# Windowed attention on pairs of tiles in four row groups, keys spread by DMA, and an expert pipeline with one more stage

## The reference

```
x = x + attention(layernorm(x))     # 16 heads of 8, token i sees tokens i-31 .. i
x = x + ffn(layernorm(x))
attention: qkv = h @ W_qkv + b_qkv; softmax(q k^T / sqrt(8), window 32) v; @ W_out + b_out
ffn:       shared expert: (h @ ws_up * silu(h @ ws_gate)) @ ws_down, for every token
           router: softmax(h @ w_router) over 8; only the first choice counts;
           choices 0 to 6: + 2 * p * ((h @ w_up[e] * silu(h @ w_gate[e])) @ w_down[e])
           choice 7: nothing is added
```

## Time and profile before

| | us |
|---|---|
| median of 3 runs | 367.87 (359.6 to 368.02) |
| the profiled execution | 365.89, its span 364.2, mean granted clock 0.986 |
| first find_max to the end of the last weigh_values | 21.6 to 151.2 |
| scatter on POOL begins | 176.9 |
| experts' first full step to the last | 247.9 to 349.2 |

### The profile page before, as it was taken

How to read it: one execution, slowest core, us unless ns; L and a number is a source line. 1 busy time by engine, 2 the same in 40 slices (tenths; PEclk the granted TensorE clock), 3 DMA queues, 4 the chain that set the end, 5 groups by cost and what they waited for, 6 DMA issues and landing times. The chain is left out here.

```text
span 364.2 us, 12603 instructions
## 1 busy us (share of the span) xinstructions
PE 323.2 (89%) x4976; PEld 251.8 (69%) x4976; DVE 226.5 (62%) x539; ACT 173.5 (48%) x313; POOL 175.6 (48%) x256
## 2 busy tenths in 40 slices
PE   8878999989889888997794799998899999999980
PEld 8645665655646555796682688876788888888870
DVE  4975888888788978779552133344555555555540
ACT  1646657557556755854231122233455445445530
POOL 6652456464446646785477244463333334333331
PEclk9999999999999999999999899999999999999996
DMA  8964433333443321000013111132343443433200
GB/s 205 354 226 126 123 104 99 100 98 97 133 119 103 99 50 38 4 2 0 22 54 114 50 61 60 63 65 67 60 77 74 79 75 66 80 74 69 62 17 0
DMA packets 56844, 30.68 MB, mean 84 GB/s; under 512 B 27073, under 2 KB 53189, under 8 KB 56787
## 3 DMA queue, kind: packets, MB, share of 16 engines
q1 hardware_dynamic: 53216, 23.18, 25.7%
q0 software_dynamic: 2880, 6.43, 5.1%
q10 hardware_dynamic: 690, 0.26, 0.4%
HBM read 13.72 MB, written 11.95 MB: 70 GB/s over the span
## 5 line engine op out<-in xcount | busy, mean ns | idle before, releaser
L608 POOL DMA_INDIRECT out<-y,xn_base x38 | 37.5, 986 | 69.9 <-DVE y L1220 69.9
L1233 DVE TENSOR_TENSOR Pr<-psS,PT 128x256 f32<-128x256 f32 x76 | 28.7, 420 | 41.4 <-issue 29.5
L892 DVE TENSOR_REDUCE row_max<-psS 128x16 fp32r<-128x1024 f32 x32 | 39.1, 1224 | 17.7 <-PE psS L1294 17.7
L1036 DVE TENSOR_TENSOR hT<-psS,PT 128x512 f32<-128x512 f32 x32 | 22.1, 690 | 40.7 <-PE psO L1456 20.5
L777 ACT ACTIVATE PT<-psS 128x512 f32<-128x512 f32 x32 | 19.1, 597 | 57.3 <-PE psS L1444 24.9
L1580 PEld LDWEIGHTS psB<-down_sb,Pr 128*128 128x128 f32 x304 | 39.6, 191 | 5.5 <-issue 2.4
L437 POOL TENSOR_TENSOR rows<-rows,proj 128x128 f32<-128x128 f32 x31 | 14.1, 456 | 57.3 <-ACT proj L686 54.8
L1580 PE MATMUL psB<-down_sb,Pr 128*128 x304 | 40.2, 275 | 1.8 <-DVE y L1220 1.0
L928 DVE STREAM_TRANSPOSE PT<-Pr 128x1024 f32<-128x1024 f32 x32 | 39.6, 1236 | 2.6 <-ACT Pr L680 2.4
L1323 PEld LDWEIGHTS psO<-VD,PT 128*32 128x32 f32 x2048 | 22.4, 109 | 25.0 <-issue 24.5
L1323 PE MATMUL psO<-VD,PT 128*32 128x36 f32 x2048 | 26.6, 200 | 10.8 <-DMA VD<-V 7.0
(11 more groups left out here) (200 smaller groups left out, 724.2 us busy)
## 6 DMA issues: line engine op xcount, KB each, us to landing
sorted_rows<-pad_row SPq DMA_DIRECT2D x19, 264.0 KB
VD<-V SPq DMA_DIRECT2D x120, 36.0 KB, 2.4
xn_base<-sorted_rows SPq DMA_DIRECT2D x38, 66.0 KB
xs<-sorted_rows SPq DMA_DIRECT2D x152, 16.0 KB
rows<-in_L_attn_x SPq DMA_DIRECT2D x8, 256.0 KB, 5.7
gate_sb<-in_L_ffn_w_gate SPq DMA_DIRECT2D x1, 1792.0 KB, 10.3
up_sb<-in_L_ffn_w_up SPq DMA_DIRECT2D x1, 1792.0 KB, 14.9
down_sb<-in_L_ffn_w_down SPq DMA_DIRECT2D x7, 256.0 KB
```

Source lines behind the costliest of these rows:

```text
L608: pool.indirect_dma_start(out=out_list, out_offset=bass.IndirectOffsetOnAxis(tok_u[:, r, :], 0), in_=y[:, r, :], in_offset=None, bounds_ch ...
L892: nc.vector.tensor_reduce(row_max[:, k % 2, :], s, AX.X, ALU.max).then_inc(max_done, 1)
L1233: nc.vector.tensor_tensor(hs[:, r % 2, h], psS[:, r % 2, h], sg[:, r % 2, h], ALU.mult).then_inc(done, 1)
```

## The change

**Pairs and row groups.** Attention goes by pairs of tiles. The queries are evicted once. Head h of each group of 4 now lies on partitions h, h+4, ... of the group's 32 (a permuted copy of the weights, `wqk_sb`), and each score matmul uses 32 rows and 32 columns of the array, so that 16 tiles of the array are named in turn. A pair has 16 mask matmuls and 32 score matmuls, over all four banks of `psS`. The next pair's scores wait for both exponentials of this one.

**Keys.** From the second batch on ACT evicts the keys once into `K`, and four DMAs on SP copy each head's rows into `Kx`, whose other rows stay zero. A batch's first scores wait for them (`k_in`).

**SP's order.** Downs and padding leave the places between the spreads and stand behind the last one: 10 padding DMAs (the last is shorter), then the 7 downs. The padding's source is made by POOL in the memory of V, once all spreads have landed.

**PE's order** in a pair, and the experts': a whole gate and up of tile s, then the transposes of s-1, then down of s-2.

```diff
-                for v in range(2):
-                    last = nc.scalar.activation(
-                        Qx[:, odd, v, :], psA[:, :], ACT.Identity, bias=bq_of[:, v : v + 1], scale=pair_of[:, v : v + 1]
-                    )
+                nc.scalar.activation(
+                    Qx[:, odd, :], psA[:, :], ACT.Identity, bias=bqk_sb[:, 0:1], scale=1.0
+                ).then_inc(q_ready, 1)
...
+            def evict_k(n, odd):
+                act.wait_ge(k_done, n + 1)
+                if n > 0:
+                    if n > 1:
+                        act.wait_ge(k_in, 16 * HPG * (n - 1))
+                    nc.scalar.activation(
+                        K[:, :], psB[:, :], ACT.Identity, bias=bqk_sb[:, 1:2], scale=1.0
+                    ).then_inc(k_ready, 1)
+                    return
...
+            def spread_keys(n):
+                sp.wait_ge(k_ready, n + 1)
...
+                for h in range(HPG):
+                    sp.dma_start(Kx[h::HPG, n % 2, h, BLK:], K[h::HPG, :]).then_inc(k_in, 16)
...
-            for n in range(B):
-                for half in range(2):
-                    spread_values(n, half)
-                    load_or_pad()
-                    load_or_pad()
+            spread_values(0, 0)
+            spread_values(0, 1)
+            for n in range(1, B):
+                spread_keys(n)
+                if n > 1:
+                    spread_values(n - 1, 1)
+                spread_values(n, 0)
+            spread_values(B - 1, 1)
+            sp.wait_ge(pad_ready, 2)
+            for lo in range(0, MT, PADS):
+                write_pads(lo, min(lo + PADS, MT))
+            for e in range(NE):
+                load_down(e)
...
+            mm(psB[:, 0:2], by_dim[:, :], bqkv_sb[:, 0:2], start=True, stop=True).then_inc(bqk_mm, 1)
...
+            act.wait_ge(bqk_mm, 1)
+            nc.scalar.copy(bqk_sb[:, :], psB[:, 0:2]).then_inc(bqk_ready, 1)
+            act.wait_ge(bqk_ready, 1)
             normalise_first()
...
+                for t in range(TPP):
                     for j in range(NJ):
-                        at = k * P + j * BLK
-                        for t in range(2):
-                            r = slice(2 * t * BLK, 2 * (t + 1) * BLK)
...
+                        at = (h * TPP + t) * P + j * BLK
+                        for g in range(NG):
+                            r = slice(g * BLK, (g + 1) * BLK)
                             last = mm(
...
+                                psG[j * BLK : (j + 1) * BLK, g, t * HPG * KEYS : (t + 1) * HPG * KEYS],
+                                Qx[r, b % 2, at : at + BLK], Kx[r, b % 2, :, at : at + KEYS],
+                                start=False, stop=True, skip_group_check=True,
                             )
...
+            for p in range(NP):
+                find_max(p, 0)
+                find_max(p, 1)
+                if p > 0:
+                    output(p - 1)
+                turn_probs(p, 0)
+                turn_probs(p, 1)
...
+            for s in range(1, MT):
+                expert_gate(s, s, at[s])
+                expert_up(s, s, at[s])
+                if s + 1 < MT:
+                    [at[s + 1]] = weights_of(s + 1)
+                expert_turn(s - 1, s - 1)
+                if s >= 2:
+                    expert_down(s - 2, s - 2, at.pop(s - 2))
```

More of the change, by code:

```diff
@@ L756, in batch @@
[L756 to L768 removed]
+                if p > 0:
+                    evict_proj(p - 1)
@@ new lines, in pair @@
+                if n < B and h == 0:
+                    evict_q(n, odd, first=n < 2)
+                if n + 1 < B and h == 1:
+                    evict_xnT(n + 1)
+            for p in range(NP - 3):
+                pair(p)
+            normalise_rows(3, 1)
+            pair(NP - 3)
+            normalise_rows(4, 1)
+            turned_batch(0)
+            turned_batch(1)
+            pair(NP - 2)
+            turned_batch(2)
+            turned_batch(3)
+            pair(NP - 1)
+            turned_batch(4)
@@ L982, in batch, with turn_probs @@
-            def batch(b, first=False, last=False):
-                for k in range(TPB):
-                    tile(b, k, first=first, last=last)
-            find_max(0, 1, first=True)
-            batch(0, first=True)
-            for b in range(1, B - 1, 2):
-                batch(b)
-                batch(b + 1)
-            batch(B - 1, last=True)
-            output(B - 1, TPB - 1)
+            def turn_probs(p, half):
+                dve.wait_ge(exp_done, p * HALVES + half + 1)
+                if p > 0:
+                    dve.wait_ge(pv_done, p * TPP)
+                nc.vector.transpose(PT[:, half, :], Pr[:, half, :]).then_inc(pt_done, 1)
@@ L1359, in _ @@
             pe.wait_ge(filled, after["masks"])
[L1360 to L1365 removed]
+            pe.wait_ge(zeros_ready, 2)
+            scores(0)
             pe.wait_ge(bias_ready, 1)
@@ L1512, in _ @@
-            batch(B - 2, 0, edge="next")
-            batch(B - 1, 1, edge="last")
+            shift_scores(0, 0)
+            shift_scores(0, 1)
+            turn_x(1)
+            scores(1)
+            keys(1)
+            queries(1)
+            for p in range(1, NP):
+                b, h = divmod(p, PPB)
+                n = b + 1
+                weigh_values(p - 1, 0)
+                if n == B:
+                    turn_rows(2 * h + 1)
+                elif h == 0:
+                    keys(n)
+                else:
+                    values(n)
+                shift_scores(p, 0)
+                weigh_values(p - 1, 1)
+                shift_scores(p, 1)
+                if p >= NP - 3:
+                    turn_rows(2 * (p - NP + 3))
+                elif h == 0:
+                    queries(n)
+                else:
+                    turn_x(n + 1)
+                project(p - 1)
+                if p + 1 < NP:
+                    scores(p + 1)
@@ L1514, in _ @@
+            route_wide()
+            pe.wait_ge(weights_split, 4)
+            pe.wait_ge(shared_in[2], 16)
+            shared_up(0, 0, first=True)
+            for t in range(TPP):
+                weigh_values(NP - 1, t)
             shared_up(0, 1, first=True)
-            project(B - 1, TPB - 1)
+            project(NP - 1)
             turn_rows(5)
```

613 lines of the change are left out of this document (251 added, 362 removed).

## The result

| | before | changed |
|---|---|---|
| median of 20 runs each | 367.41 us (359.6 to 371.54) | 366.07 us (363.94 to 369.23) |
| the profiled execution | 365.89 us, span 364.2 | 365.95 us, span 364.2 |
| mean granted clock of the profiled execution | 0.986 | 0.967 |
| ratio, and its 95% interval | | 1.0087 (1.0054 to 1.012) |

No change at 2%, with a small loss where I had forecast a gain of 1.3% (363 against the 367.9 of the first three runs). The ratio counts only executions within 1.5% of their kernel's fastest, and the kernel before has a wide spread with 359.6 at its lower end; that is why the ratio is above 1 while the medians are not. On the two other chips on which both kernels were timed side by side, the medians agree with the ratio: 354.92 against 358.75 us, ratio 1.0075 (1.0029 to 1.0122), and 354.95 against 357.7, ratio 1.0139 (1.0066 to 1.0212).

What follows compares the result with a forecast made beforehand. The prediction took SP's DMA queue to bound attention. From 365.9 us for the profiled execution, +0.4 for attention and -3.5 for the experts gave 362.8, so 363; range 353 to 372, the forecast's own 358 to 368.

Steps and rivals of the forecast that it cites:

- SP's queue sets the length of attention: Attention: SP issues DMAs without pause, 20 a batch at 0.80 us, 16.0 us, where compute could do 14.5.
- The 26.2 us beyond the bare issues: SP in attention: time left above 97.3 us of bare issues, put down to long issues and kept in the new sum.
- They are fetches of instructions: SP's long issues in attention, about one in 4.6 us, are instruction fetches and should stay as frequent.
- The end of attention: Last issue at 147.2, landing 2.5 us later, both last tiles weighed by 151.3; with +0.3 behind, attention +0.4 us.
- The start: ACT's first normalisation waits for the bias matmul and an eviction, 0.6 us together; first spread +1.1 us.
- the clock falls: Rival for attention: PE, with less work and waits in one lump, loses clock; 17 us slower, 380; chance 0.07.
- The experts: Expert steps: 2.65 us instead of 2.77, 35 × 0.12 = 4.2, less 0.7: -3.5 us, bounds -1 and -5.
- All that compute saves is hidden, the chain of a pair is 13.8 a batch: Attention: compute savings lie behind SP's queue; a pair takes 6.9 us, 13.8 a batch, leaving 2.2 us of cover.
- Keys' new wait: Attention: the next batch's key DMAs wait 5.0 us for K, barely covered by 8 spreads, 5.1 us bare.
- Padding and downs at nothing: Behind attention: padding starts near 151, needs 45 us at 104 GB/s, downs come behind it; nothing late, 0.
- crowded DMAs: Rival behind attention: padding and downs, 7 MB at once, slow all engines around 151 to 171; 7 us, 370; chance 0.18.
- A key DMA with half the runs costs half: SP in attention: by the skill's small-transfer rule, 32 runs cost half of 64, ending attention some 8 us sooner.

Runs made afterwards that it cites:

- e2: The kernel before with its 26 DMAs of padding and downs moved behind the last spread: 347.16 us, ratio 0.9807 to the kernel before.
- e5: The changed kernel with each key DMA split in two of half the tokens, 56 instead of 28: 378.65 us, ratio 1.0655 to the kernel before.
- c1: The kernel before, unchanged, timed against itself on another chip: ratio 0.9982.
- c4: The changed kernel, unchanged, one look on the same chip as a look at the kernel before: single execution of 359.2 us.
- c5: The changed kernel, unchanged, timed again on the chip of e9: 357.7 us, ratio 1.0139 to the kernel before.
- e8: e4 with the expert stage of the kernel before: 349.89 us, ratio 0.9857 to the kernel before.
- e9: The changed kernel with the bias matmul placed before the last 32 of 128 warm-up matmuls: 355.45 us, ratio 1.0064 to the kernel before.
- e10: e8 with the early bias matmul of e9: 348.94 us, ratio 0.9892 to the kernel before.
- c2: The changed kernel, unchanged, timed on another chip: 358.75 us, ratio 1.0075 to the kernel before.
- e6: The changed kernel with its last expert step in the old order: 358.36 us, against 358.75 for the changed kernel on the same chip.
- e3: The changed kernel with keys evicted by four ACT activations ahead of the exponentials, no key DMAs: 358.02 us, ratio 1.0108 to the kernel before.
- e4: The changed kernel without key DMAs, keys by four activations behind the exponentials, values' matmuls and eviction also moved back: 349.57 us, ratio 0.9858 to the kernel before.
- e1: The kernel before with the changed kernel's expert stage alone: 354.51 us, ratio 1.0001 to the kernel before.
- e11: The kernel before with padding and downs behind the last spread, as e2, beside e10: 348.16 us, ratio 0.9886 to the kernel before.

## Why the prediction was wrong

- **"SP's queue sets the length of attention": right**, and so was the price of a key DMA (0.64 from start to start; measured 2.42 to 2.46 for four without a long issue among them, 0.59 of issue). e2 took 26 DMAs off the queue and attention ended 8 us sooner; e5 put 28 on and it ended 21.7 us later.
- **The 26.2 us beyond the bare issues: on the high side.** Worked out as in the prediction, they are 22.0 to 26.7 us in four traces of the old attention and 20.8 to 25.1 in five of the new (SP's own waits are in them, 3.8 us in c1). In the mean the queue grew by 1.1 us, about two DMAs at 0.64, not by 2.5.
- **"They are fetches of instructions": borne out.** The long issues don't come from the padding: 21 spreads took over 0.75 us in the first trace before, 22 in c1, and 21 in e2, without padding among them. They do come with the packets of the instruction queue. This is that queue within SP's stretch, in the first trace before and then in e5 (packets, MB, share of 16 engines):

```profile
q8 instruction: 27, 0.44, 1.7%
```

```profile
q8 instruction: 27, 0.44, 1.4%
```

In the first trace 27 of the 154 issues took over 0.75 us, and each of the 27 packets lies on one of them. In e5, whose stretch is 19 us longer, it is again 27 packets, and 26 long issues. Over all 18 traces 431 of the 433 long issues overlap a packet, where of the short ones about one in six does, and in the first trace before, the first changed one, e2 and e5 about half of the long issues end 0.36 to 0.39 us after their packet. What holds SP's issue up meanwhile, the trace doesn't show.

- **The end of attention: a wrong step.** I let the last `weigh_values` end 4.1 us after the last issue, from landing and weighing. It ends 7.6 to 9.0 us after it in the traces of the old attention and 6.9 to 8.1 in those of the new: a whole pair's chain stands there, and in PE's program the first six matmuls of the shared expert (145.5 to 147.0 us in the first changed trace). So of the 3.5 us that I let this change save there, 0.8 are found in the mean (8.3 us before, 7.4 now), and with +1.6 at the start and +1.1 in the queue that makes the +1.9 at attention's end, where I had +0.4.
- **The start: too large for an undisturbed trace, too small on average.** I took +1.1; it is +0.7 in the first pair of traces and +1.6 in the mean. The step "it now waits 0.6 us" left out that PE idles 1.93 us behind its own warm-up, where it idled 0.9 at most before. In 4 of 9 traces with that wait (c4, c5, e5, e8) the granted clock then fell to 0.50 to 0.60 at 15 to 17 us, and the first spread came at 22.5 to 22.9 us. In e9 and e10 the gap was shorter, and both were absent.
- **The rival "the clock falls": too dear, but its mechanism was there.** It asked for a low clock through all of attention, and the window of the earlier trace rows has 1.00. Yet each of the six traces with the changed attention (the first, c2, c4, c5, e6, e9) has one or two stretches at half clock between 87 and 142 us, most of them behind just the wait in one lump that the rival named. c4, PE in order of time, and the stretch behind it:

```profile
87.93 0.77 PE L1319 MATMUL psO<-VD,PT 128*32 128x36 f32 x64 [1.99 <-DMA VD<-V]
```

```profile
88.90:92.30 3.40, 3.40 (x68) 1.74 (x67) 0.00 (x0) 1.66 (x2) 0.27 (x1) 0.51 0.21 50
```

The waits before such a stretch are 1.5 to 3.2 us; others as long passed without one (2.9 us at 137 in c5). None of the seven traces with the old attention has one between 34 and 166 us, and neither has any of the four without key DMAs (e3, e4, e8, e10). Over all executions the mean granted clock is 0.972 (c2) and 0.974 (c5) on chips on which the kernel before has 0.984 and 0.987; in the four kernels without key DMAs it is 0.982 to 0.983. What these stretches cost attention was not separated from the queue's own length.

- **The experts: the step that failed most.** I forecast -3.5; it is +0.7 to +1.3 on the later chips (and -0.35 between the first two traces). Three errors. The step is 2.72 to 2.73 and not 2.65, because transposes ahead of a down take 0.43 where ahead of a gate they take 0.37, so that only the small waits are gained (0.05 a step in e1, not 0.12). The clock had no term: on the later chips PE's waits in the first steps are gathered into one of 2.4 to 2.8 us, and the clock falls behind it in nine traces of nine, which costs 1.7 us by the estimate under e1, about the difference between -0.35 and +1.1. And the drain costs 1.8, not 0.7: one more down, and its wait, behind the last gate; the down itself, 0.8 us, comes back in the first steps, which hold one less.
- **"All that compute saves is hidden, the chain of a pair is 13.8 a batch": the first half right, the figure wrong.** With SP free, pairs come at 14.8 to 15.0 us a batch and tiles at 14.4 to 14.5. With SP relieved, attention ended 8 us sooner (e2 against c1, e4 against c2), not the 13 us of one rival.
- **Keys' new wait: covered, as said.** PE's waits for the scores of a batch were 1.4 us in all in the first trace, at the first of them.
- **Padding and downs at nothing: right.** From the last weighing to the first scatter it takes 25.5 to 25.7 us in every trace, with them there or not (25.56 in c1, 25.63 in c2). The prediction's 45 us for 5.1 MB at 104 GB/s should read 49, which changed nothing.
- **The rival "crowded DMAs"** fell with it. The clock of 0.81 in 188 to 206 us goes with "remote" stalls, which the kernel before has too.
- **"A key DMA with half the runs costs half": no.** That estimate of 8 us was not in the sum. A key DMA's issue has 0.59 us as median, a spread's 0.60.

## What to carry over

Count what stands on the queue that bounds a stage, item by item, and test it by moving items away and by doubling them; here 26 DMAs that nobody needed yet cost more than all the matmuls, evictions and reductions that a new attention layout saved. A software pipeline one stage deeper moves work and waits to its ends: count the downs, the waits and the clock of the fill and the drain against the gain per step before trusting it. And a wait that a change makes longer, or gathers from two into one, can cost more than its own length, since the clock may fall behind it: look at the granted clock behind each such wait, in several traces.

## What the runs showed of the hardware

- **Chips differ by 11 us in one stage.** On the first chip the stage from the first scatter to the second gate took 71.0 and 73.2 us, with "remote" stalls on ACT and DVE at once. On four others, 16 traces of both kernels' forms took 59.8 to 62.0 there, and none had such a stall beside the same scatters. What the engines wait for isn't in the trace. It stays open; leaving the scatters out was not tried, since no later run fell on a chip that had the stalls.
- **The clock after a gap of 1.93 us is not certain.** It was lost in four traces and kept in five. With gaps of 1.20 us (e9) and 0.12 (e10) it was kept. After the single wait of 2.4 to 2.8 us among the first experts it was lost in nine traces of nine. From 20 to 30 us, where PE waits 2.3 to 2.6 us for the first row maxima, it was 0.83 to 0.88 in every trace of the changed attention but one with 0.68 (e10), and 0.98 to 1.00 in those of the old, where that wait is 1.2 us, but for two with 0.83 (e1, e11).
- **One fall costs 1.8 us where PE is busy.** It is the difference between 59.8 and 61.6, and between 60.2 and 62.0, from the first scatter to gate 1, in traces that differ there in the clock.
- **Long issues on SP come with the packets of the instruction queue,** 431 of 433 in 18 traces; each packet has 16 KB and takes 0.9 to 1.9 us.
- **The price of an issue goes by the DMA, not by what it carries:** the issue of half a key DMA on SP has the same median as that of a whole one, 594 ns, and 28 more made SP's stretch 15.0 us longer beside its waits, 0.54 each.
